# One more key tile for TensorE in a later group's first block, one fewer in a group's last block, and the last denominators behind the second output projection

## What is computed

```
q = qkv[..., :D_MODEL].reshape(B, S, HEADS, HEAD_DIM)
k = qkv[..., D_MODEL:D_MODEL + HEAD_DIM]
v = qkv[..., D_MODEL + HEAD_DIM:]
scores = jnp.einsum('bqhd,bkd->bhqk', q, k) * scale
scores = jnp.where(causal[None, None], scores, min_val)
attn = jax.nn.softmax(scores, axis=-1)
ctx = jnp.einsum('bhqk,bkd->bqhd', attn, v)
out = jnp.einsum('bsd,ed->bse', ctx.reshape(B, S, D_MODEL), out_w) + out_b
x = _layernorm(x + out)
```

## Time and profile before

| | before |
|---|---|
| median of three runs | 1117.82 us (1116.93 to 1120.11) |
| the profiled execution: its time | 1121.4 us |
| its span, first to last instruction | 1119.7 us |
| mean granted clock of PE | 0.993 |
| PE busy | 1079.0 us |
| DVE busy | 888.6 us |
| ACT busy | 713.4 us |
| POOL busy | 199.3 us |

### The profile page before, as it was taken

How to read it: one execution, slowest core, us unless ns; L and a number is a source line. 1 busy time by engine, 2 the same in 40 slices (tenths; PEclk the granted TensorE clock), 3 DMA queues, 4 the chain that set the end, 5 groups by cost and what they waited for, 6 DMA issues and landing times.

```text
span 1119.7 us, 17340 instructions
## 1 busy us (share of the span) xinstructions
PE 1079.0 (96%) x5970; PEld 520.2 (46%) x5994; DVE 888.6 (79%) x1101; ACT 713.4 (64%) x844; POOL 199.3 (18%) x162
## 2 busy tenths in 40 slices
PE   8999999999999999999989999999999999999996
PEld 6365435543337433335634643474333654333462
DVE  4566899779976699987667679976998767898956
ACT  6734785478864498885445457644888447888821
POOL 3520332013110120111032013301211201211000
PEclk9999999999999999999989999999999999999999
DMA  4976401442001622001352353016400152200001
GB/s 146 208 114 141 124 1 40 106 121 38 2 2 53 137 76 38 1 1 39 78 136 75 75 131 76 2 52 138 113 1 1 39 126 65 38 1 2 1 1 38
DMA packets 40331, 72.19 MB, mean 64 GB/s; under 512 B 13969, under 2 KB 14993, under 8 KB 40209
## 3 DMA queue, kind: packets, MB, share of 16 engines
q1 hardware_dynamic: 24624, 56.64, 19.1%
q0 software_dynamic: 13584, 11.54, 7.1%
q10 hardware_dynamic: 2000, 2.51, 0.7%
HBM read 25.58 MB, written 8.39 MB: 30 GB/s over the span
## 4 chain that ended last, share of the span: by engine, by line
PE 75%; DVE 12%; issue 5%; ACT 2%; POOL 2%; DMA 1%; SPq 1%; DVEq 0%; ACTq 0%; POOLq 0%
PE sc L1184 21%; PE bank L1206 19%; PE sc L1037 8%; PE bank L1037 7%; PE sc L1327 7%; DVE psum_k L833 5%; PE sc L1224 3%; PE sc L1342 2%; PE bank L1224 2%; DVE stats L909 2%; POOL prob L520 1%; DVE res L906 1%; PE bank L1335 1%; PE sc L1271 1%; PE bank L1342 1%
## 5 line engine op out<-in xcount | busy, mean ns | idle before, releaser
L653 ACT ACTIVATE prob<-sc 128x1024 f32<-128x1024 f32 x544 | 525.5, 1025 | 133.7 <-PE sc L1184 133.5
L833 DVE TENSOR_TENSOR psum_k<-psum_k,prob 128x2048 f32<-128x2048 f32 x170 | 403.4, 2373 | 4.7
L1184 PE MATMUL sc<-q_st,k_st 128*128 128x512 f32 x1088 | 327.1, 422 | 8.0 <-DVE rden L882 3.8
L1184 PEld LDWEIGHTS sc<-q_st,k_st 128*128 128x128 f32 x1088 | 183.7, 188 | 249.7 <-ACT prob L653 177.3
L1206 PE MATMUL bank<-prob,v_sb 128*32 128x512 f32 x2176 | 288.2, 607 | 3.3 <-POOL prob L520 3.3
L520 POOL TENSOR_SCALAR_AFFINE_SELECT prob<-prob 128x1024 f32<-128x1024 f32 x64 | 112.4, 1798 | 527.7 <-ACT prob L653 527.7
L1327 PE MATMUL sc<-prob,w_sb 128*128 128x512 bf16 x503 | 117.3, 379 | 1.3 <-issue 1.3
L1206 PEld LDWEIGHTS bank<-prob,v_sb 128*32 128x32 f32 x2176 | 44.5, 108 | 107.4 <-issue 89.4
L683 ACT ACTIVATE prob<-sc 128x512 f32<-128x512 f32 x64 | 38.0, 594 | 73.0 <-PE sc L1327 72.9
L833 DVE TENSOR_TENSOR psum_k<-prob 128x2048 f32<-128x2048 f32 x28 | 64.0, 2286 | 20.7 <-POOL prob L520 17.1
L1037 PE MATMUL bank<-q_st,wq_hi 128*128 128x512 f32 x240 | 80.3, 399 | 0.0
(11 more groups left out here) (160 smaller groups left out, 1017.5 us busy)
## 6 DMA issues: line engine op xcount, KB each, us to landing
q_st<-q_hi SPq DMA_DIRECT2D x120, 128.0 KB, 2.4
q_st<-q_lo SPq DMA_DIRECT2D x120, 128.0 KB, 2.4
res<-in_x SPq DMA_DIRECT2D x8, 1024.0 KB, 5.3
res<-ob_sb POOLq DMA_DIRECT2D x8, 1024.0 KB, 9.5
out_x<-res SPq DMA_DIRECT2D x32, 256.0 KB, 2.1
res<-in_xT SPq DMA_DIRECT2D x7, 1024.0 KB, 5.0
w_sb<-in_w POOLq DMA_DIRECT2D x8, 256.0 KB, 9.1
prob<-in_wqkvT ACTq DMA_DIRECT2D x4, 288.0 KB, 6.1
```

Of the source, the lines that this page charges most:

```text
L653: nc.scalar.activation(prob[t % NP][:, half * HW:(half + 1) * HW], score_half(q // TB, 2 * t + half).rearrange("p m n -> p (m n)"), ACT.Ex ...
L833: nc.vector.tensor_tensor(acc[:, :], first[:, :], prob[t % NP][:, :], ALU.add).then_inc(add_v, 1)
L1184: last = nc.tensor.matmul(dst, k_st[:, k * P:(k + 1) * P], q_st[slot][:, c * HJ:(c + 1) * HJ, at:at + P], start=True, stop=not shift)
```

## The change

`BY_PE` gets one more in the first block of groups 1 to 3 (blocks 4, 8, 12) and one fewer in the last block of each group (3, 7, 11, 15):

| block q | 3 | 4 | 7 | 8 | 11 | 12 | 15 |
|---|---|---|---|---|---|---|---|
| tiles left to PE before | 1 | 1 | 1 | 1 | 2 | 2 | 2 |
| tiles left to PE now | 0 | 2 | 0 | 2 | 1 | 3 | 1 |

What PE no longer sums, DVE adds, and the other way round. The denominators of a group's last block also move behind the output projection of the group's second block.

```
-BY_PE = [0] + [1] * 9 + [2] * (NQ - 10)
+BY_PE = [0] + [(1 if q < 10 else 2) + (q % TB == 0) - (q % TB == TB - 1) for q in range(1, NQ)]
...
                 def finish_attention(g):

+                    project_out(g, 1)
                     denominators(TB * (g + 1) - 1)
-                    project_out(g, 1)
                     project_out(g, 2)
```

## The result

The changed kernel took 1136.46 us (median of 4 runs, 1135.84 to 1137.14), the kernel before 1118.96 us beside it (4 runs, 1116.93 to 1120.48). The ratio is 1.015 (95% interval 1.0135 to 1.0165), 17.5 us more. The forecast was 1133.8 us, with a range from 1122 to 1140.5 us.

The account below looks back on a forecast made before the run. PE's own queue was taken to bound the kernel. First blocks +6.4, ends +6.2 and clock +3.4 us gave +16.0 us on the 1117.8 us median: 1133.8 us, range 1122 to 1140.5 us.

Parts of the forecast that it names:

- Block 8: the wait goes, the part comes: At block 8, PE's 0.69 us wait for DVE's last addition goes and the added part comes: 0.
- DVE holds group 2: Rival: DVE limits group 2, so the addition removed at block 8 frees PE; 1111.5 us, half 1114.7; chance 0.04.
- Block 12, +2.4 us: Per sequence at block 12: added part 0.86 us, plus 1.5 us waiting for tile 94's exponentials, held by the denominators.
- Turns, not shares: At group ends, DVE's additions and POOL's large subtraction block each other for whole instructions; L833 over 6 us in group 1.
- The second rival: DVE and POOL share instead of taking turns, and no clock falls: +4.7 us, 1122.5 us; chance 0.12.
- End of group 1, +2.4 and +1.4 us: PE waits for DVE's fifth addition, held behind POOL: +2.4 us in the first sequence, +1.4 in the second.
- Group 2, -0.55 us each: At group 2's end DVE's addition beats POOL by 0.07 us; PE saves 0.86, 0.3 comes back: -0.55 us.
- the first rival: Turns hold, POOL wins both group 2 races, clock falls longer at three places: up to 1143 us; chance 0.13.
- Ends of group 3, +1.55 and +1.8 us: First sequence: PE waits for DVE's addition behind POOL, +1.55 us; second: later denominators delay DVE's layernorm, +1.8 us.
- The clock, +3.4 us at two of three places: PE's clock halves after long waits at ends of groups 1, 1 and 3: 1.7 us at two of three.
- Group 0: End of group 0: -0.9 us in first sequence, POOL being late; +1.0 in second, second L901 waiting for POOL.
- The fourth: Rival: waits cancel the parts within what can be measured, ends or block 12 free; about 1119 us; chance 0.08.

Follow-up runs that it names:

- e5: The changed kernel with block 12's denominators three tiles behind its last tile instead of four: 1131.94 us, ratio 1.0119 to the kernel before.
- e3: The changed kernel, but block 12 keeps two tiles for PE as before: 1133.60 us, ratio 1.0136 to the kernel before.
- e4: The changed kernel, with POOL's large subtraction waiting for DVE's last addition of the group and third block's rounding rest: 1126.29 us, ratio 1.0069 to the kernel before.
- e8: The changed kernel without tiles added to first blocks and with the old order in the last sequence's last group: 1126.30 us, ratio 1.0064 to the kernel before.
- e7: Same as e8, plus POOL's large subtraction waiting for DVE as in e4: 1115.41 us, ratio 0.9968 to the kernel before.
- e2: The changed `BY_PE` table, with the last denominators left where they stood in the kernel before: 1144.41 us, ratio 1.0221 to the kernel before.
- e1: The kernel before with its own table, only the last denominators moved behind the second output projection: 1123.56 us, ratio 1.0046 to the kernel before.
- e6: Control: the kernel before, with POOL's large subtraction waiting for DVE as in e4: 1119.35 us, ratio 1.0004 to the kernel before.

## Why the prediction was right, and where it was off

- **PE bounds the kernel, and a part costs 0.86 us.** Right: block 4 cost 0.8 us in both sequences.
- **Block 8: the wait goes, the part comes.** Right, 0.0 us, and the two waits of `sc` L1224 are gone. So the rival "DVE holds group 2" is ruled out: its 2.29 us did not come.
- **Block 12, +2.4 us.** The mechanism held (e5), the size was 2.1: the waits were 1.22 and 0.18 us against 1.15 and 0.35, and the step had no term for the wait of 0.46 us for the mask, which went (gone in the changed kernel and in e5, there in e3).
- **Turns, not shares.** Right: 6.54, 6.56 and 6.59 us for an addition behind POOL, 6.67 us for POOL behind an addition; e4 and e8 against e7 show that this is worth 10 to 11 us of time. The second rival falls with it. (Its sum gave back 3.5 us at seven ends; 7 x (0.86 - 0.3) is 3.9 us, which would put it at 1122.1 us.) The Trainium skill ("SBUF — State Buffer", section "Who interferes with whom") says that issue order decides who fully blocks; this case's traces agree, down to an advantage of 0.07 us.
- **End of group 1, +2.4 and +1.4 us.** The waits came as described. In the first sequence 1.41 us of PE's wait was moved to 180.53, where nothing that the trace shows ends it, and 0.5 us more came later. PE's wait for the addition alone was 1.53 us there, not 3.3; with the 1.41 us it is 2.9. The second sequence cost +1.4 us up to its third projection, as predicted, and the clock behind it another 1.2 us.
- **Group 2, -0.55 us each.** Right: -0.5 and -0.4 us. DVE won by 0.07 us, the margin that was worked out. It was not luck: POOL's subtraction takes 6.67 to 6.70 us at all ten ends of group 2 in the five traces with that addition and without POOL's wait (the changed kernel, e2, e3, e5, e8). So the first rival's condition never came.
- **Ends of group 3, +1.55 and +1.8 us.** +2.0 and +2.7 us. Up to L1271 the last group cost 1.95 us (from the first projection on, 18.75 us before and 20.70 us after), as the step says; the other 0.8 us is the clock behind the wait of 1.91 us, a place for it that the step did not have.
- **The clock, +3.4 us at two of three places.** This was the term with the weakest ground. It fell at one of the three, behind the longest wait (3.22 us), and not behind 2.29 us; it cost 1.2 us there and 0.8 us in the last group, 2.0 us in all. Which of the places is hit is not fixed by the wait: at the third, with the same wait, it fell in e3 and e5. The sign named for it, digits below 9 in `PEclk`, did not come and could not in slices of 28.4 us.
- **What no term had.** The start of group 3's attention cost +1.3 and +0.8 us. DVE's pause of 1.0 to 1.3 us ahead of L910 is in the changed kernel and in e2, e3, e4 and e5, all with the added tiles of blocks 4 and 8, and not in the kernel before, e1, e6, e7 and e8, which lack them. What it is stays open: no run took it apart. Loading of instructions is one candidate that the traces neither show nor rule out: a packet of an instruction queue (q14 on the page) ends 0.2 to 0.4 us ahead of each of the ten pauses, but one ends 0.2 to 0.5 us ahead of the same instruction in the five kernels that do not pause, too.
- **Group 0.** -2.1 us in the first sequence instead of -0.9, and -0.5 instead of +1.0 in the second. The end of the second cost +0.9 us, as the step says. The other 2.7 us belongs to this pair of executions: the clock of the one of before fell at 63.8 and for 6.8 us at 579.3, that of the changed kernel's at 37.4 and for 3.4 us at 586.97. Two other traces show it. e5 has the changed kernel's code but for block 12's denominators, and e6 that of before but for POOL's wait, at which PE loses nothing; in both the clock stays in group 0 of the first sequence and falls for 3.4 us at the start of the second. Between them group 0 costs -0.6 and +0.8 us, together the 0.1 us that was forecast. In the first sequence there is luck in that: the step had no wait for the rounding rests behind the new addition (0.89 us, 1.71 us in e5), and it costs little only because PE stood idle there before as well (2.06 us, 2.02 us in e6).
- **The other rivals.** The fourth, by which the waits cancel the parts, would need about 1119 us. It is ruled out by the ratio's interval.
- **A small size.** A projection costs PE 2.9 us from start to start, not 2.8 (1073.46 to 1076.37 in the last group of the changed kernel).

So 1133.8 us was 2.7 us low. Of this 1.1 us is the base: the median of before was 1117.82 us in the runs shown and 1118.96 us in the later ones. The other 1.5 us is the sum, 16.0 against a timed difference of 17.5. In the profiled pair the difference was 14.4 us, 1.6 below the sum; with group 0's 2.7 us, which belongs to that pair alone, it is 17.1. Against the sum that leaves two terms too high, block 12 by 0.6 and the clock by 1.4 us, one missing, the start of group 3's attention with 2.0 us, and some 1.1 us of small ones at the ends of groups 1, 2 and 3. The steps held one by one, but that the total came so close is in part luck: what was put too high and what was missing are 2.0 us each.

## What to carry to other kernels

Where two engines take turns, as DVE and POOL did here, work moved from PE to one of them is priced by what the other does at that moment: 2.29 us of addition became 6.5 us three times, and turned a saving of 0.86 us of PE into a wait of up to 3.2 us. Look for such an instruction on the other engine first, and if its result isn't needed soon, hold it back until the urgent one is done: that cost nothing in a kernel where nobody waited (e6) and was worth 10 us where PE did (e4, and e7 against e8). When a step is moved behind something as cover, ask of each place whether there is anything behind it too: in the last group there wasn't, and it made most of what the order alone lost (3.6 of 5.0 us).

## What the runs showed of the hardware that I had not expected

- The two engines' turns are decided by hundredths of a microsecond. DVE came 0.07 us before POOL at 331.93 and had its 2.29 us; at 178.54, 1.2 us behind POOL, it had 6.54 us.
- A waiting POOL gets its turn at the next end of a DVE instruction, even with another DVE instruction 0.04 us behind it: DVE's additions end at 178.50 and start at 178.54, and it is POOL that runs then, to 182.92.
- PE's clock did not follow the length of the wait just ahead alone: it fell behind 1.49 and 1.91 us (36.82, 1094.16) and stayed behind 2.29 us (529.51). The same wait can go either way. At the end of group 3 it stayed behind 2.29 us in the changed kernel and fell behind 2.23 and 2.21 us in e3 and e5. At the first wait for a DMA it fell behind 1.49 us (the changed kernel) and 1.28 us (e8), and stayed behind 1.51 us (e7, at 36.53). Each fall shifts a stretch by 1 to 2 us in one trace and not in the other, so two traces are to be compared with their clocks beside them.
- Pauses that the trace ends by "issue" move with the program: PE's 2.06 us of the earlier trace rows is gone (PE waits 0.89 us for DVE at that place), one of 1.41 us stands at 180.53, and DVE's of 1.0 to 1.3 us came with the added tiles in five kernels of five.
